# A four-layer graph network on one core: counts summed as int16, the mask on another queue, and work of three engines in other places

## What is computed

```python
x = _layernorm(x + L0(x, edge_index, edge_weight))     # attention with 8 heads, masked by edges, then a feed-forward product
x = _layernorm(x + relu(segment_sum(h[src] * norm)))   # L1, h = x @ W; norm from the degrees, with 512 loops more
x = _layernorm(x + L2(x, edge_index, edge_type_4))     # four relations: messages, mean over the incoming edges, gelu feed-forward
x = _layernorm(x + L3(x, src, dst))                    # attention over edges (softmax by target), relu feed-forward
```

## Time and profile before

| | |
|---|---|
| median of 3 runs | 583.27 us (582.19 to 585.47) |
| the profiled execution | 581.37 us, its span 579.6 us |
| PE, PEld busy | 530.0 us (91%), 351.7 us (61%) |
| DVE, ACT, POOL busy | 396.6 us (68%), 225.9 us (39%), 282.2 us (49%) |
| mean granted clock of PE | 0.973 |

### The profile page before, as it was taken

The page is one execution under the profiler, slowest core; times in us unless marked ns, Lnnn a source line. Parts: engine busy times, 40 slices in busy tenths (PEclk is TensorE's granted clock), DMA queues, the critical chain, the costliest instruction groups (busy, mean ns, idle before and its releaser), DMA issues.

```text
span 579.6 us, 7779 instructions
## 1 busy us (share of the span) xinstructions
PE 530.0 (91%) x2524; PEld 351.7 (61%) x2524; DVE 396.6 (68%) x939; ACT 225.9 (39%) x473; POOL 282.2 (49%) x271
## 2 busy tenths in 40 slices
PE   6999999999969999898899999997998997999880
PEld 2444444448845545666677888877876785555750
DVE  6996979999947769974676744464427626774846
ACT  2120530017227662574441233143534226765443
POOL 6557556668457777404342600066653654766000
PEclk8999999999989999998999999998999999999996
DMA  7940000000665210226632500028652852100001
GB/s 239 400 151 1 1 1 0 0 0 2 198 199 166 55 37 1 73 60 157 213 115 82 178 31 1 0 81 248 182 182 73 259 171 69 47 2 1 0 0 73
DMA packets 29913, 54.37 MB, mean 94 GB/s; under 512 B 4962, under 2 KB 6446, under 8 KB 29368
## 3 DMA queue, kind: packets, MB, share of 16 engines
q1 hardware_dynamic: 15964, 27.14, 15.0%
q0 software_dynamic: 11968, 19.96, 11.5%
q10 hardware_dynamic: 1948, 6.86, 3.5%
HBM read 51.78 MB, written 2.17 MB: 93 GB/s over the span
## 4 chain that ended last, share of the span: by engine, by line
PE 47%; DVE 10%; ACT 5%; POOL 5%; DMA 4%; issue 3%; ACTq 0%; DVEq 0%; POOLq 0%
PE bank L498 9%; PE bank L499 8%; PE bank L500 8%; PE bank L616 4%; PE bank L600 4%; PE bank L591 3%; POOL wl L346 3%; DMA wh<-w_o 2%; PE bank L693 2%; PE bank L691 2%; PE bank L692 2%; DVE h L1084 2%; DVE h L1083 1%; PE bank L568 1%; PE bank L484 1%
## 5 line engine op out<-in xcount | busy, mean ns | idle before, releaser
L346 POOL TENSOR_TENSOR wl<-wraw,wh 128x512 fp32r<-128x512 f32 (+1 forms) x78 | 105.4, 1372 | 81.1 <-ACT x L811 14.9
L521 PE MATMUL bank<-hot 128*128 128x512 bf16 x544 | 119.5, 383 | 2.5 <-DVE hot L1132 2.5
L521 PEld LDWEIGHTS bank<-hot 128*128 128x128 bf16 x544 | 53.5, 99 | 68.7 <-DVE hot L1132 4.1
L387 POOL DMA_INDIRECT edge_bias<-ewn,cell_at x68 | 75.1, 1105 | 40.4 <-issue 20.2
L498 PE MATMUL bank<-wh,tl 128*128 128x512 f32 x176 | 71.3, 405 | 0.6 <-DVE tl L1043 0.5
L499 PE MATMUL bank<-wl,th 128*128 128x512 f32 x176 | 69.4, 395 | 0.0
L500 PE MATMUL bank<-wh,th 128*128 128x512 f32 x176 | 69.4, 394 | 0.0
L819 ACT ACTIVATE sp<-sp,peak 128x512 f32<-128x512 f32 x44 | 31.8, 722 | 26.4 <-DVE peak L1255 26.1
L1132 DVE TENSOR_SCALAR hot<-iota,pair_dst,digit 128x1024 bf16<-128x1024 f16 x68 | 41.4, 609 | 0.0
L498 PEld LDWEIGHTS bank<-wh,tl 128*128 128x128 f32 x176 | 33.5, 190 | 11.8 <-issue 4.2
L1114 DVE SCALAR_TENSOR_TENSOR eq<-keyb,key,later 128x384 f16<-128x384 f16 (+1 forms) x68 | 39.8, 609 | 0.0
(11 more groups left out here) (194 smaller groups left out, 1072.2 us busy)
## 6 DMA issues: line engine op xcount, KB each, us to landing
wraw<-w SPq DMA_DIRECT2D x26, 256.0 KB
wh<-w POOLq DMA_DIRECT2D x6, 1024.0 KB, 6.1
keyb<-edge_keys ACTq DMA_DIRECT2D x4, 1088.0 KB, 11.4
wh<-w_rel POOLq DMA_DIRECT2D x4, 1024.0 KB, 5.8
wraw<-w_rel SPq DMA_DIRECT2D x16, 256.0 KB
wraw<-w_qkv SPq DMA_DIRECT2D x8, 256.0 KB
wraw<-w_o SPq DMA_DIRECT2D x8, 256.0 KB
wh<-w_o POOLq DMA_DIRECT2D x2, 1024.0 KB, 8.0
```

Of the source, the lines that this page charges most:

```text
L346: pool.tensor_tensor(wl[n % WSLOTS][:, k, 0:width], wraw[:, q % 3, 0:width], wh[n % WSLOTS][:, k, 0:width], ALU.subtract).then_inc(s["w_lo ...
L387: pool.indirect_dma_start(out=bias_dram, out_offset=bass.IndirectOffsetOnAxis(ap=cell_at[:, c:c + 1], axis=0), in_=ewn[:, c:c + 1], in_off ...
L521: mm = pe.matmul(ps(name)[:], hot[:, slot, 0, i * P:(i + 1) * P], hot[:, slot, 1 + kind, :], start=False, stop=last, skip_group_check=True)
```

## The change

- The buffers: `call` and `call2` go; the counts are summed in int16 in two halves, `call_a` in the place of the fifth row of `par`, `call_b` in that of `iota`. `ident_r` is the identity in float32r.
- The first loads come in another order, DVE makes `ef` ahead of `row_key`, and `key` after the first chunks; POOL starts on `nbias` when two chunks are built.
- SP reads the mask back, behind `raw(7)`, instead of POOL; `cast(3)` is ahead of `low(2)`.
- DVE sums the counts (`call_sum`: one half ahead of the copies of v, one behind the loop of attention), ACT makes `cph` right behind attention, DVE `cpl` (`call_low`); PE turns `cpl` and `cph` by matmuls with `ident_r`, added in PSUM.
- Six `par` rows are loaded by SP ahead of `raw` of the last quarter of w2_self, five of them until now by ACT.
- `cast(11)`, `low(11)`, `cast(12)`, `low(12)` are ahead of POOL's residual of layer 2.
- Around the turns of layer 3 the order on PE, ACT and DVE is another, and in the last two norms tile i+1 is centred before tile i goes on.

```diff
@@ -161,3 +161,5 @@
         ident = sb("ident", [P, P], F32)
-        iota = sb("iota", [P, 2 * N], F16)
+        early = region([("iota", [P, 2 * N], F16)], [("call_b", [P, 2, N], I16)])
+        iota = early["iota"]
+        ident_r = sb("ident_r", [P, P], F32R)
         const = sb("const", [P, 4], F32)
@@ -197,3 +199,4 @@
         tl = sb("tl", [P, K, N], F32R)
-        par = sb("par", [P, 5, D], F32)
+        pars = region([("gap9", [P, 4 * D], F32), ("call_a", [P, 2, N], I16)], [("par", [P, 5, D], F32)])
+        par, call_of = pars["par"], (pars["call_a"], early["call_b"])
         add2 = sb("add2", [P, D], F32R)
@@ -208,4 +211,3 @@
         cc = region([("hot", [P, RING, 3, N], BF16), ("packed", [P, 8, N], F32), ("later", [P, WINDOW * P], F16), ("eq", [P, GROUP, WINDOW * P], F16)],
-                    [("call", [P, T, N], F32), ("cph", [P, T, N], F32R), ("cpl", [P, T, N], F32R), ("waste", [P, N], F32)],
-                    [("gap3", [P, T, N], F32), ("call2", [P, T, N], F32)],
+                    [("gap10", [P, T, N], F32), ("cph", [P, T, N], F32R), ("cpl", [P, T, N], F32R), ("waste", [P, N], F32)],
                     [("hidh", [P, 8, N], F32R), ("hidl", [P, 8, N], F32R)],
@@ -279,5 +281,5 @@
             eng = sp_
-            eng.dma_start(er[:], edge_rows.rearrange("a c p -> c a p")).then_inc(s["ld_rows"], 16)
-            eng.dma_start(ei[:], edges.rearrange("a p c -> p a c")).then_inc(s["ld_edge"], 16)
             eng.dma_start(iota[:], iota_d.to_broadcast([P, 2 * N])).then_inc(s["ld_iota"], 16)
+            eng.dma_start(ei[:], edges.rearrange("a p c -> p a c")).then_inc(s["ld_edge"], 16)
+            eng.dma_start(er[:], edge_rows.rearrange("a c p -> c a p")).then_inc(s["ld_rows"], 16)
             eng.dma_start(later[:], later_d).then_inc(s["ld_later"], 16)
@@ -290,2 +292,5 @@
 
+            def load_par(slot, name):
+                eng.dma_start(par[:, slot, :], rows_of[name].to_broadcast([P, D])).then_inc(ld_par[slot], 16)
+
             def raw(q):
@@ -305,3 +310,3 @@
                 raw(q)
-            for slot, name in ((0, "b0_v"), (1, "c0_2"), (2, "g0_1"), (3, "c0_1"), (4, "g0_2")):
+            for slot, name in ((0, "b0_v"), (1, "c0_2"), (2, "g0_1"), (3, "c0_1")):
                 eng.dma_start(par[:, slot, :], rows_of[name].to_broadcast([P, D])).then_inc(ld_par[slot], 16)
@@ -309,2 +314,5 @@
             eng.wait_ge(s["dups_done"], 1)
+            for k in range(WINDOW):
+                eng.wait_ge(scattered[k], 16 * len(range(k, CHUNKS, WINDOW)))
+            eng.dma_start(nbias[:], by_tile(bias_dram)).then_inc(s["bias_loaded"], 16)
             eng.wait_ge(s["bias_loaded"], 16)
@@ -312,2 +320,15 @@
             for q in range(8, len(QUARTERS)):
+                if q == QUARTERS.index((6, 3)):
+                    eng.wait_ge(s["cph_ready"], T)
+                    eng.wait_ge(s["cpl_ready"], T)
+                    load_par(4, "g0_2")
+                    eng.wait_ge(s["res_ready"], T)
+                    load_par(1, "b1")
+                    eng.wait_ge(normed[0], T)
+                    load_par(2, "g2_1")
+                    load_par(3, "c2_1")
+                    wait_freed(eng, ("v0", 3))
+                    load_par(0, "g2_2")
+                    eng.wait_ge(summed[2], T)
+                    load_par(4, "c2_2")
                 raw(q)
@@ -370,2 +391,3 @@
 
+            pool.wait_ge(s["hot_ready"], 2)
             pool.memset(nbias[:], -8.0 * MASK).then_inc(s["bias_init"], 1)
@@ -389,8 +411,4 @@
                                         bounds_check=CELLS - 1, oob_is_err=False).then_inc(scattered[c % WINDOW], 16)
-            low(2, (0, 1, 2))
-            for k in range(WINDOW):
-                pool.wait_ge(scattered[k], 16 * len(range(k, CHUNKS, WINDOW)))
-            pool.dma_start(nbias[:], by_tile(bias_dram)).then_inc(s["bias_loaded"], 16)
-            low(2, (3,))
             cast(3)
+            low(2)
             low(3)
@@ -402,12 +420,3 @@
             next_residual(0, 1)
-
-            for i in range(T):
-                cut = slice(i * P, (i + 1) * P)
-                pool.wait_ge(s["call_halves"], i + 1)
-                link(pool.tensor_tensor(call[:, i, :], call[:, i, :], call2[:, i, :], ALU.add))
-                pool.tensor_tensor(call[:, i, cut], call[:, i, cut], ident[:], ALU.add).then_inc(s["call_ready"], 1)
             cast(6)
-            for i in range(T):
-                pool.wait_ge(s["cph_ready"], i + 1)
-                pool.tensor_tensor(cpl[:, i, :], call[:, i, :], cph[:, i, :], ALU.subtract).then_inc(s["cpl_ready"], 1)
             cast(7)
@@ -423,2 +432,6 @@
             low(10)
+            cast(11)
+            low(11)
+            cast(12)
+            low(12)
             pool.wait_ge(s["bias3_ready"], T)
@@ -427,8 +440,4 @@
                 pool.tensor_tensor(y[:, i, :], x[:, i, :], par[:, 4, :], ALU.add).then_inc(s["res_ready"], 1)
-            cast(11)
-            low(11)
-            cast(12)
             cast(13)
             pool.wait_ge(normed[4], T)
-            low(12)
             low(13)
@@ -639,5 +648,7 @@
                 begin(("countsT", i))
-                pe.wait_ge(s["call_ready"], T)
+                pe.wait_ge(s["cpl_ready"], T)
                 for j in range(T):
-                    mm = pe.transpose(ps(("countsT", i))[:, j * P:(j + 1) * P], call[:, j, i * P:(i + 1) * P], ident[:])
+                    target, cut = ps(("countsT", i))[:, j * P:(j + 1) * P], slice(i * P, (i + 1) * P)
+                    pe.matmul(target, cpl[:, j, cut], ident_r[:], start=True, stop=False)
+                    mm = pe.matmul(target, cph[:, j, cut], ident_r[:], start=False, stop=True)
                 finish(mm, ("countsT", i))
@@ -742,6 +753,6 @@
             second_half(2)
-            turn(3, x, 6, 0)
             first_half(3)
-            turn(3, x, 6, 1)
+            turn(3, x, 6, 0)
             second_half(3)
+            turn(3, x, 6, 1)
             w_ready(15)
@@ -890,2 +901,5 @@
             roots_next()
+            act.wait_ge(s["call_summed"], T)
+            for i in range(T):
+                act.copy(cph[:, i, :], call_of[i // 2][:, i % 2, :]).then_inc(s["cph_ready"], 1)
             deviation(0, 0, h[:, 0, :])
@@ -894,5 +908,2 @@
             deviation(0, 2, h[:, 2, :])
-            for i in range(T):
-                act.wait_ge(s["call_ready"], i + 1)
-                act.copy(cph[:, i, :], call[:, i, :]).then_inc(s["cph_ready"], 1)
             turned(0, 1)
@@ -926,10 +937,2 @@
             deviation(2, 3, h[:, 3, :])
-            act.wait_ge(s["res_ready"], T)
-            load_par(1, "b1")
-            act.wait_ge(normed[0], T)
-            load_par(2, "g2_1")
-            load_par(3, "c2_1")
-            load_par(4, "c2_2")
-            wait_freed(act, ("v0", 3))
-            load_par(0, "g2_2")
             scaled_rows(3)
@@ -1000,6 +1003,6 @@
             deviation(6, 1, h[:, 1, :])
-            turned(3, 0)
             deviation(5, 2, h[:, 2, :])
-            turned(3, 1)
+            turned(3, 0)
             deviation(6, 2, h[:, 2, :])
+            turned(3, 1)
             deviation(5, 3, h[:, 3, :])
@@ -1030,5 +1033,7 @@
                 act.copy(hidh[:, f, :], hidden[:, f, :]).then_inc(s["hidh_ready"], 1)
-            for i in range(T):
+            deviation(8, 0, h[:, 0, :])
+            for i in range(1, T):
                 deviation(8, i, h[:, i, :])
-                deviation(9, i, h[:, i, :])
+                deviation(9, i - 1, h[:, i - 1, :])
+            deviation(9, T - 1, h[:, T - 1, :])
 
@@ -1099,5 +1104,2 @@
 
-            dve.wait_ge(s["ld_rows"], 16)
-            dve.scalar_tensor_tensor(out=row_key[:], in0=er[:, 1, :], scalar=float(N), in1=er[:, 0, :], op0=ALU.mult, op1=ALU.add)\
-                .then_inc(s["row_keys"], 1)
             dve.wait_ge(s["ld_edge"], 16)
@@ -1105,4 +1107,6 @@
             src, dst, typ = ef[:, 0, :], ef[:, 1, :], ef[:, 2, :]
-            link(dve.scalar_tensor_tensor(out=key[:], in0=dst, scalar=float(N), in1=src, op0=ALU.mult, op1=ALU.add))
             link(dve.tensor_scalar(high_pair[:], typ, 2.0, None, ALU.is_ge))
+            dve.wait_ge(s["ld_rows"], 16)
+            dve.scalar_tensor_tensor(out=row_key[:], in0=er[:, 1, :], scalar=float(N), in1=er[:, 0, :], op0=ALU.mult, op1=ALU.add)\
+                .then_inc(s["row_keys"], 1)
             link(dve.scalar_tensor_tensor(out=pair_dst[:], in0=high_pair[:], scalar=float(N), in1=dst, op0=ALU.mult, op1=ALU.add))
@@ -1150,2 +1154,3 @@
                 link(dve.memset(const[:, n:n + 1], value))
+            link(dve.scalar_tensor_tensor(out=key[:], in0=dst, scalar=float(N), in1=src, op0=ALU.mult, op1=ALU.add))
             dve.sem_inc(s["const_ready"], 1)
@@ -1170,2 +1175,3 @@
             link(dve.tensor_scalar(second[:], second[:], -1.0, None, ALU.mult))
+            link(dve.tensor_copy(ident_r[:], ident[:]))
             dve.wait_ge(s["ld_bias"], 64)
@@ -1237,4 +1243,15 @@
```

(71 more changed lines are left out.)

4 lines of the change are left out of this document (removed).

## The result

569.51 us median (569.0 to 569.88, four runs), against 582.89 of the kernel before; ratio 0.9759, 95% interval 0.972 to 0.9798: 2.4% faster. The profiled execution took 569.0, its span 566.1 (before 581.37 and 579.6). That lies in the range of 552 to 573, but 7.5 above the number, and the sum did not hold term by term.

What follows compares the result with a forecast made beforehand. PE works 91% of the span, so only its waits, the half clock behind them, head and tail can be won; 0.5 + 4.5 + 6.4 + 3.9 + 1.8 + 3.5 = 20.6 us gained gave 562, range 552 to 573.

Steps and rivals of the forecast that it cites:

- Start: Kernel start, reordered loads and POOL's later `nbias`: first counting matmul near 6.3, 0.5 us gained, bounds 3.6 gained to 2 lost.
- the prediction's own signs of being wrong: PE waiting for `hot` after the start, PE waiting at v0, or over 2 us at L600.
- The rival of held DVE: Everywhere: DVE is held at every meeting with POOL, gains sum to only 13.2 us, time 569; chance 0.27.
- First attention: `cast(3)` first and SP reading the mask shorten the wait for softmax scaling: 6.3 us less 1.8 charged, 4.5 kept.
- the 1.8 charged for `call_sum(1)`: First attention: cost taken off because the count sum on DVE, ahead of the v0 copies, meets `low(3)`.
- the slow rival: First attention: v0's weights come late behind `cast(3)`, PE stands 10.4 us, 585.5 in all; chance 0.05, 0.03 of it slower.
- Counts and two norms: Count sums off POOL, transposes as matmuls and `par` loads on SP gain 2.7 + 2.1 + 1.6 = 6.4 us.
- The 32 narrow matmuls: Counts: they replace 16 transposes at the same width, some 3.8 us, 1.9 more; 5.4 more at the 512-column price.
- The `par` loads: Ahead of the last normalise: ACT's five loads cost 2.07 us, and the half clock behind the wait 1.6.
- the sum of the counts taken off POOL: Counts: DVE no longer held under POOL's subtractions, after the extra matmuls and `call_sum(0)`'s meeting 2.7 us gained.
- w2_1a and turns: w2_1a's splits ahead of the residual gain 2.3 plus 1.6 of clock, 3.9 us; layer 3's turns gain 1.8.
- Last norms: Kernel tail: centring the next tile early ends it at 573.7 instead of 577.2, 3.5 us gained.

Runs made afterwards that it cites:

- s1: The changed kernel without POOL's wait for two built chunks, so POOL starts on `nbias` at once: 561.86 us, ratio 0.9674.
- s2: The changed kernel with DVE's scaling of the edge weights (`ewn`) put right behind the first four chunks: 569.44 us, ratio 0.9784.
- s3: The changed kernel with POOL's DMA issue of `nbias` put behind its seven subtractions instead of ahead: 562.69 us, ratio 0.9677.
- t_par: The changed kernel with the whole start of the kernel before, and the five later `par` loads issued by ACT again: ratio 0.9667.
- t_low: The changed kernel with the whole start of the kernel before, and w2_1's splits behind POOL's residual again: ratio 0.9729.
- t_mask: The changed kernel with the start of before and POOL's old order behind the scatters (v's splits, mask read, then w_o's cast last): ratio 0.9707.
- v_spread: Two runs of the changed kernel, with old and new start, POOL's splits spread one by one between the scatters: ratios 0.973 and 0.9701.

## Why the prediction was right, and where it was not

*Start: the step that failed.* "Bounds: 3.6 us gained to 2 lost. I take 0.5": measured 8.0 lost. The first counting matmul came at 6.88, not near 6.3, and two of the prediction's own signs of being wrong appeared: PE waited for `hot` after the start (9.3), and ahead of v (1.0). The step took the builds held at 13.80 (1.50 instead of 0.54) as the price of a meeting and put POOL's work onto them, one by one. It had the other price in its own rows, 5.66 for four subtractions, used it as a rival, and there too at only 1.5 us for the start. It found the 5.66 in agreement with a lock held for one instruction; but one of POOL's four subtractions there takes 1.25 (4.99 in all), so 5.66 is already more than that. What it did not ask is which DVE instruction begins while POOL issues the DMA that stands right ahead of seven subtractions with all their data there. By moving `nbias` behind the first chunks the change puts that issue at 12.7 to 13.7 instead of 7.3 to 8.4, where POOL then idled until 12.25. s1, s2 and s3 show this link by link: another issue time, another victim, another place of the issue.

The rival of held DVE gave 569, and 569.5 was measured, but not by its account: it had start -1.5, attention 0, counts 5.5, and the stages have -8.0, 4.5, 6.8. It named the mechanism and put it in the wrong place.

*First attention: 4.47 for 4.5, by errors that cancel: luck.* The wait for scores fell from 5.35 to 0.53, and the clock behind it was 1.00 (174 to 182), as forecast. Nothing of the 1.8 charged for `call_sum(1)` was paid: it ran at 165.7 to 168.4, and `low(3)` began at 169.19. Its additions take half of what a float32 one of that length would:

```profile
L1248 DVE TENSOR_TENSOR call_b<-call_b,counts x1: 693/693/693, 166.4 to 166.4; 128x1024 int16<-128x1024 int16 x1
```

0.69 us for 1024 int16 elements, as for 512 of float32: the lower end of that step. (The other half, which meets POOL's residual, took 1.64 an addition.) The Trainium skill (VectorE: DVE Perf Modes, The perf-mode tier table) gives 16-bit `tensor_tensor` two elements a cycle; the trace agrees. In its place PE lost 1.0 at v and 0.3 more at `deg_rows` (1.08, before 0.74); 0.6 more is not attributed. The wait at v is the slow rival in small: `low(2)` behind `cast(3)`, `raw(7)` asked for at 154.57 and its split only at 160.44.

```profile
161.76 0.50 PE L507 MATMUL bank<-wh,tl 128*128 128x512 f32 x1 [0.98 <-POOL wl L367]
```

*Counts and two norms: 6.78 for 6.4.* The 32 narrow matmuls took from 237.90 to 241.67, the 3.8 costed by their width, and behind them no DVE operation is held by POOL (0.75 at 238.74 and 240.99). The `par` loads are worth 1.6 by t_par, not 3.7. The clock of 268 to 272 is back at 1.00 all the same, and stays so in t_par with the loads put back, so something else in the stage keeps it up; what, was not told apart. Of the 6.8, 5.2 are left beside these 1.6. The clock is some 1.7 of them (0.43 x 4), and the rest, 3.5 where 2.7 was costed, falls to the sum of the counts taken off POOL, which no run tests alone.

*w2_1a and turns: 6.75 for 5.7.* The wait of 3.4 for `wl` became one of 1.6 for the turned tile: 1.8, costed at 2.3. t_low puts the step at 5.6 instead of 3.9: the clock behind the wait was undersized, 3.2 instead of 1.6. That leaves 1.2 for the turns, costed at 1.8; no run tests them alone. *Last norms: 3.5*, to the tenth, in both directions (G).

## What to carry to other kernels

Before moving work of GpSimd, look where each of its DMA issues falls and what stands right behind it: a run of its tensor operations with no wait between them, directly behind an issue, can hold one small VectorE instruction for the whole run, and whoever waits for VectorE stands with it. A gap, a wait or another place of the issue turns the same overlap into turns of a microsecond. And where VectorE has little to spare, work of GpSimd spread over it one by one, each piece right behind a DMA issue, was dearer than in one place where a queue of finished work covered it.

## What the runs showed of the hardware beyond what was expected

- In the fourteen traces a single VectorE instruction lasted over 3 us five times: 4.71 (at 143.74) and 5.66 (at 236.73) before, 9.43 after, 9.15 in s2, 4.7 in t_mask. Each time it had begun during a GpSimd DMA issue that tensor operations followed within 0.04 us, and it ended 0.06 to 0.6 behind the last of them. The 22 splits of the two v_spread runs show the same with runs of one (1.79 to 2.34). Begun in the middle of such a run an instruction got in at the next boundary: `ewn` took 0.77 and 0.90 (s1, s3) instead of 0.20, builds 1.29 to 1.49 instead of 0.35 and 0.54. The Trainium skill (SBUF — State Buffer, Who interferes with whom) has the shared pair held for a whole instruction; the begins in the middle agree with that, and the 9.43, seven instructions, goes beyond it.
- The hold begins with the issue and not with the first tensor operation: `ewn`, begun at 12.91, needs 0.20 when free, so it would have been through 0.6 before the subtractions began at 13.71. But an issue with nothing right behind it held nothing: before the change the builds at 7.31 and 7.58, during the issue of 7.28 to 8.44, took 0.35 and 0.54. Nor is each begin ahead of a run caught: where two issues stood one behind the other (151.76 in the kernel after) it took 1.64, and a `memset` took 0.27 (s2, 13.54). Why the issue decides was not found.
- The same wait of 2.3 us for the same rows came with a clock of 0.57 behind it before and with 1.00 in t_par.
